# State-space scan: 5 of 16 input products on GpSimd from B rows spread by DMA, parts of B and C in a ring through DRAM, and an out-projection that alternates images

## The reference

```python
x = x + conv_branch(group_norm(x))           # 4 images, S = 1024 positions, 384 channels
t = tokens(x); t = t + attention(layer_norm(t)); t = t + experts(layer_norm(t))

def conv_branch(x):
    xh, z = split(x @ in_proj_w.T)           # 192 channels each
    xc = silu(depthwise_3x3(xh) + conv_b)
    xs = [xc by rows, xc by columns, both reversed]          # K = 4 directions
    dt, B, C = split(x_proj_w[k] @ xs[k], [24, 16, 16])      # N = 16 states
    delta = softplus(dt_projs_w[k] @ dt + dt_projs_b[k])
    for t in range(1024):                    # for each direction, channel and state n
        h[n] = h[n] * exp(delta[t] * A[n]) + delta[t] * x[t] * B[n, t]
        y[t] += C[n, t] * h[n]
    y = sum of the 4 directions, put back in order, + D * x
    y = layer_norm(y) * g + b
    return (y * silu(z)) @ out_proj_w.T      # back to 384 channels
```

## Time and profile before

| | us |
|---|---|
| median of 3 runs | 2788.26 (2787.69 to 2788.27) |
| the profiled execution's own time | 2789.66 |
| its span, first to last instruction | 2787.9 |
| TensorE matmuls busy | 2276.9 (82%) |
| TensorE weight loads busy | 1034.7 (37%) |
| VectorE busy | 1734.4 (62%) |
| ScalarE busy | 1189.9 (43%) |
| GpSimd busy | 1160.4 (42%) |
| mean granted TensorE clock | 0.927 of full |

### The profile page before, as it was taken

One profiled execution on the slowest core, in us unless ns is written; L12 is line 12 of the kernel. 1 busy time (PEld: TensorE's weight loads), 2 busy tenths in 40 slices (PEclk: granted clock), 3 DMA queues, 4 the chain that ended last, 5 costly groups with the idle time before them and its releaser, 6 DMA issues.

```text
span 2787.9 us, 21841 instructions
## 1 busy us (share of the span) xinstructions
PE 2276.9 (82%) x6404; PEld 1034.7 (37%) x6404; DVE 1734.4 (62%) x1497; ACT 1189.9 (43%) x1301; POOL 1160.4 (42%) x551
## 2 busy tenths in 40 slices
PE   4887877778787777778777776889988649999998
PEld 2333323323332333333233322444455425555554
DVE  2436999999999999999999997752122200000000
ACT  1226666666676666657666664211111111111111
POOL 0002767776676777667676764000000141111111
PEclk9988999999999999999999999789999769999999
DMA  5111000000000000000000002201011252222220
GB/s 193 56 25 44 1 0 1 0 0 0 0 0 0 0 0 0 0 0 0 0 0 0 0 0 108 83 34 45 1 45 45 92 189 101 102 104 102 104 101 17
DMA packets 44296, 111.04 MB, mean 40 GB/s; under 512 B 5168, under 2 KB 30883, under 8 KB 42978
## 3 DMA queue, kind: packets, MB, share of 16 engines
q1 hardware_dynamic: 38114, 93.59, 9.5%
q0 software_dynamic: 6144, 16.98, 1.7%
HBM read 74.68 MB, written 34.67 MB: 39 GB/s over the span
## 4 chain that ended last, share of the span: by engine, by line
PE 47%; issue 22%; DVE 18%; ACT 8%; POOL 3%; DMA 1%; DVEq 1%; SPq 0%; ACTq 0%; POOLq 0%
PE ps L975 9%; PE ps L987 9%; DVE ps L1123 8%; PE ps L756 5%; ACT arena L525 3%; POOL arena L385 3%; DVE arena L1131 3%; PE ps L700 3%; PE ps L939 2%; PE ps L737 2%; PE ps L825 2%; PE ps L864 2%; PE ps L711 2%; PE ps L727 2%; ACT arena L533 2%
## 5 line engine op out<-in xcount | busy, mean ns | idle before, releaser
L385 POOL TENSOR_TENSOR arena<-arena 128x1024 f32<-128x1024 f32 x384 | 975.5, 2540 | 438.4 <-DVE arena L1131 423.5
L1131 DVE TENSOR_TENSOR_SCAN arena<-arena,ps 128x1024 f32<-128x1024 f32 x384 | 878.1, 2287 | 13.3
L756 PE MATMUL ps<-arena 128*128 128x512 f32 x1536 | 777.9, 631 | 43.0 <-DVE arena L1110 40.1
L737 PE MATMUL ps<-arena 96*128 (+1 forms) x1536 | 424.3, 395 | 275.0 <-DVE arena L1131 236.2
L533 ACT ACTIVATE arena<-ps 128x1024 f32<-128x1024 f32 x384 | 392.4, 1022 | 437.6 <-PE ps L737 435.3
L1123 DVE TENSOR_TENSOR ps<-ps,arena 128x1024 f32<-128x1024 f32 x384 | 465.9, 1213 | 35.2 <-PE ps L737 32.7
L525 ACT ACTIVATE arena<-arena 128x1024 f32<-128x1024 f32 x384 | 438.5, 1142 | 0.3
L756 PEld LDWEIGHTS ps<-arena 128*128 128x128 f32 x1536 | 309.8, 203 | 313.6 <-issue 252.0
L737 PEld LDWEIGHTS ps<-arena 96*128 96x128 bf16 x1536 | 126.5, 100 | 688.5 <-DVE arena L1131 445.5
L1344 DVE TENSOR_TENSOR arena<-ps,arena 128x384 f32<-128x384 f32 x32 | 17.9, 558 | 450.2 <-PE ps L987 450.2
L987 PE MATMUL ps<-arena 128*128 128x384 f32 x768 | 250.2, 486 | 0.0
(11 more groups left out here) (166 smaller groups left out, 1708.6 us busy)
## 6 DMA issues: line engine op xcount, KB each, us to landing
arena<-in_w SPq DMA_DIRECT2D x16, 2304.0 KB, 16.1
slot_in<-arena SPq DMA_DIRECT2D x8, 772.0 KB, 16.0
arena<-slot_in SPq DMA_DIRECT2D x8, 772.0 KB, 18.4
arena<-in_xT SPq DMA_DIRECT2D x4, 1536.0 KB, 9.3
arena<-in_x_tok SPq DMA_DIRECT2D x1, 6144.0 KB, 21.5
tokens<-arena SPq DMA_DIRECT2D x4, 1536.0 KB, 5.8
out<-arena SPq DMA_DIRECT2D x4, 1536.0 KB, 9.6
z_scratch<-arena SPq DMA_DIRECT2D x4, 768.0 KB, 5.5
```

Source lines behind the costliest of these rows:

```text
L385: nc.gpsimd.tensor_tensor(hst[:, u % RING], hst[:, u % RING], c_sb[:, u % RING], ALU.mult).then_inc(p2_ok, 1)
L737: mm = pe.matmul(dst[:, h * 512:(h + 1) * 512], sel_lhs[0:BR, n], bc[0:BR, q // J, dr, m, h * 512:(h + 1) * 512], start=True, stop=True)
L756: mm = pe.matmul(Y_PS[:, h * 512:(h + 1) * 512], ident, hst[:, u % RING, h * 512:(h + 1) * 512], start=(u == 0), stop=(u == UN - 1))
L1131: nc.vector.tensor_tensor_scan(h, f, x, 0.0, ALU.mult, ALU.add).then_inc(sc_ok, 1)
```

## The change

- Units with n in `ON_POOL` = (2, 5, 8, 11, 14), 10 of the 32 of a tile, no longer get a B spread from TensorE nor a product from VectorE. SP loads their B row from DRAM into the unit's slot of `hst`, once for each half of the partitions, by a transfer that reads the row 64 times. GpSimd multiplies it there with `dux`, LEAD = 3 units ahead of its read-outs. Their decay goes to the unit's free buffer of `B_PS` in PSUM, when the scan of unit u-2 is done, and the scan takes decay from PSUM and input from SBUF, in place.
- `hst` has 8 slots (HRING), and LAG is 4: the addition trails by 4 units, and the evacuation comes at unit 4.
- The parts of B and C are stored to DRAM, and `bc` holds two groups in place of four; groups 2 and 3 are loaded when tiles 3 and 6 begin. A new ScalarE copy per projection step puts the B and C rows in fp32 into `rows`, which a seventh transfer stores to DRAM.
- The out-projection takes tile i of both images together, and alternates them matmul by matmul, into two banks of PSUM. Order: tiles 0 and 1, means, tile 2, squares, tile 3. VectorE's additions follow it.

```diff
-LAG = 3
+HRING = 8
+LAG = 4
+ON_POOL = (2, 5, 8, 11, 14)
+LEAD = 3
...
-        BCD = XY + 16 * S
+        BCD = XY + 12 * S
-        bc = rb.take(2 * NP, 2, 2, S, dtype=BF16)
+        bc = rb.take(2, 2, 2, S, dtype=BF16)
+        rows = rw.take(2, S)
-        hst, c_sb = rs.take(RING, S), rs.take(RING, S)
+        hst, c_sb = rs.take(HRING, S), rs.take(RING, S)
...
+            def load_bc(po):
+                sp.dma_start(bc[0:BR, po % 2], bc_dram[po]).then_inc(bc_ld, 16)
+
+            for p in range(NP):
                 for k in range(K):
...
-                            sp.dma_start(bc[part * SR:part * SR + SR, p * 2 + o, dr, m, :],
+                            sp.dma_start(bc_dram[p * 2 + o, part * SR:part * SR + SR, dr, m],
                                          parts[H2 + m * SR:H2 + m * SR + SR, k % 2, part]).then_inc(bc_st[k % 2], 16)
+                    sp.wait_ge(rows_ok, p * K + (k + 1))
+                    sp.dma_start(b_dram[p * 2 + o, dr], rows[H2:H2 + SR, k % 2]).then_inc(rows_st[k % 2], 16)
+                if p == 0:
+                    for o in range(2):
+                        sp.wait_ge(bc_st[o], 1 + K // 2 * PLACED)
+                    load_bc(0)
+                    load_bc(1)
+
+            def b_row(q, u):
+                dr, n = divmod(u, N)
+                sp.wait_ge(ya_ok, q * UN + u + 1)
+                for im in range(2):
+                    sp.dma_start(hst[H2 * im:H2 * im + H2, u % HRING],
+                                 b_dram[q // J, dr, im * N + n].partition_broadcast(H2)).then_inc(b_ld[u % HRING], 16)
...
+            for U in range(NQ * UN):
+                if U % UN in POOL_UNITS:
+                    b_row(U // UN, U % UN)
+                if U % (J * UN) == 0 and J * UN <= U < 3 * J * UN:
+                    sp.wait_ge(c_ok, U)
+                    load_bc(U // (J * UN) + 1)
...
+            def make_input(q, u):
+                dr, slot = u // N, u % HRING
+                pool.wait_ge(du_ok, q * 2 + (dr + 1))
+                pool.wait_ge(b_ld[slot], q * (32 * fed(slot)) + 32 * (fed(slot, u) + 1))
+                nc.gpsimd.tensor_tensor(hst[:, slot], hst[:, slot], dux[:, dr], ALU.mult).then_inc(in_ok, 1)
+
             def read_outs(q, last):
...
+                    if u + LEAD < UN:
+                        if u + LEAD in POOL_UNITS:
+                            make_input(q, u + LEAD)
+                    elif not last and u + LEAD - UN in POOL_UNITS:
+                        make_input(q + 1, u + LEAD - UN)
...
+                    nc.scalar.activation(rows[H2:H2 + SR, k % 2], SLOT3[k % 2][H2:H2 + SR], ACT.Copy).then_inc(rows_ok, 1)
...
-                    if not (first and u < RING):
-                        act.wait_ge(sc_ok, U + (3 - RING))
+                    kept = 2 if n in ON_POOL else RING
+                    dst = B_PS[u % 2] if n in ON_POOL else decay[:, u % RING]
+                    if not (first and u < kept):
+                        act.wait_ge(sc_ok, U + (3 - kept))
...
-                    pe.wait_ge(sc_ok, U + 1)
-                    spread(q, u, 0, B_PS[u % 2]).then_inc(b_ok, 1)
+                    if n not in ON_POOL:
+                        pe.wait_ge(sc_ok, U + 1)
+                        spread(q, u, 0, B_PS[u % 2]).then_inc(b_ok, 1)
...
+            def out_proj(c, i):
+                if i == 0:
+                    pe.wait_ge(yg_ok, 1 + c * J + J)
+                for r in range(2):
+                    pe.wait_ge(ta_ok, c * 8 + (OP_SEEN + 2 * i + r + 1 - OP_BACK[i]))
+                for j in range(J):
+                    for r in range(2):
+                        lo, hi = H2 * r, H2 * r + H2
+                        mm = pe.matmul(ps[:, op_bank(i, r), 0:C], yg[lo:hi, j, i * P:(i + 1) * P], w_out[lo:hi, j],
+                                       start=(j == 0), stop=(j == J - 1))
...
-                    dve.wait_ge(b_ok, U + 1)
-                    nc.vector.tensor_tensor(B_PS[u % 2], B_PS[u % 2], dux[:, dr], ALU.mult).then_inc(p1_ok, 1)
+                    h, slot = hst[:, u % HRING], B_PS[u % 2]
+                    if n in ON_POOL:
+                        f, x = slot, h
+                        dve.wait_ge(in_ok, q * len(POOL_UNITS) + (pool_units(u) + 1))
+                        dve.wait_ge(dec_ok, U + 1)
+                    else:
...
```

120 lines of the change are left out of this document (72 added, 48 removed).

## The result

The changed kernel takes 2711.63 us (median of 4 runs, 2708.24 to 2728.21) against 2788.27 us before: ratio 0.9737, 95% interval 0.9697 to 0.9777. The profiled execution took 2712.99 us, with a span of 2711.2. The time moved by 76.7 us, where 120 were forecast; it lies inside the range. A later comparison of the same kernel gave 2727.52 us (6 runs, 2707.47 to 2737.21; 0.9764, 0.9730 to 0.9798). Single executions of this kernel spread over 30 us, which those of before don't.

A forecast was written before the change was run, and what follows sets the result against it. VectorE, 97% busy in the scan stage, was taken as the bound; without stalls it would need 1284.9 us. Scan stage -121.8, projection +14, out-projection -12 gave -120 us, a median of 2668 us; range 2630 to 2722.

The forecast's parts named there:

- the 71 us: Scan stage: VectorE's delta work slows GpSimd's read-outs by 71 us in all, taken as unchanged; GpSimd's total 1291 us.
- boundary, with unit 6: Tile boundaries: VectorE waits for TensorE 3.5 us x 11 = 39, against 35 before: +4 (-20 to +15).
- decay through PSUM at unit 11: Scan stage: the exponential of GpSimd's unit 11 comes 0.2 us late, 23 times: +5 us (0 to 15).
- coupling, and loads of B and C: Scan stage: hiccups passed between equally loaded engines, +12 us (0 to 50); 768 KB loads ahead of a row, +6 (0 to 12).
- The core term: Scan stage: VectorE loses 10 products in each of 12 tiles, 120 x 1.24 = 148.8 us; scans stay at 2.287 us.
- GpSimd becomes the bound: Rival, chance 0.20: scan stage 1391 us in place of 1469, -78, and 2712 us with the other terms.
- Rows: Scan stage: B rows for GpSimd arrive in 4.2 us, landing taken as 3, against 6.3 us free; hidden by 2 us.
- Projection: Stage before the scans: new copy and seventh transfer +7 us, stores and loads about +7: +14 (0 to 22).
- Out-projection: After the scans: last chunk -7 us (21.3 to 15 or a little less), earlier chunks -5: together -12 (0 to -20).
- Alternating images should make that the rule: Out-projection: alternating images makes the two array halves work side by side, 0.64 us for a pair of matmuls.
- The signs listed for "right": VectorE above 93%, GpSimd above 90% busy, rows landing in 3 to 5 us, half-tiles 55 to 57, projection steps near 6.1.
- those for "wrong": Scan stage: late GpSimd inputs over 30 us, its products above 2.5, scans not 2.287, TensorE below 0.9 clock, or long exponentials.

The follow-up runs named there:

- N1: Changed kernel with GpSimd's units counted on the product's semaphore too, so all three waits before a scan compare with one value; 2723.08 us, ratio 0.9760.
- the images in turn: Changed kernel with the out-projection's three products of image 0 ahead of those of image 1, instead of alternating; 2729.29 us, ratio 0.9777.

## Why the prediction was right in sign and 43 us too far

**The step that failed** is this one: "What slows GpSimd is delta work, whose operations take both inputs from SBUF ... so I let the 71 us stand". It counted the contention on the engine that used to lose, and took VectorE's own delta operations as fixed at 0.59 + 3 x 1.12 us a half-tile. The trace of before could show it on one side only, because GpSimd idled for the scan and came second each time. With GpSimd 93% busy, VectorE comes second in most half-tiles. The same sentence priced GpSimd's total well (1291 us; L453, L439 and dux together 1312) and the loss on VectorE's side at 0 instead of 54. That these 54 us come from GpSimd's products is shown by the run without the 120 input products for 42 of them; the other 12 are argued.

The Trainium skill has this rule: SBUF — State Buffer, section Who interferes with whom, says that a VectorE instruction with two SBUF inputs contends with a GpSimd instruction that reads SBUF, that the pair of ports which both engines share is an exclusive lock, and that "Issue order, not op shape, decides who blocks." The rows agree (1.0 us to go gave 0.88 more, 0.30 gave 0.18). That an operation of VectorE waits through two further products of GpSimd that follow one another, as at 991.29, is measured here.

**The terms of the stage**, against VectorE's 1284.9 us without a stall:

| | forecast | measured |
|---|---|---|
| boundary, with unit 6 | 39.7 | 26.7 |
| decay through PSUM at unit 11 | 5 | 0.6 |
| coupling, and loads of B and C | 18 | 1.1 (what is left) |
| delta operations | 0 | 54.3 |
| pitch from product to scan | 0 | 36.7 |
| sum | 1347.6 | 1404.3 |

- The core term, 120 products x 1.24 us, held: 264 products of 1.214 us are left, and scans with decay in PSUM take 2.270 us, not the 2.287 assumed.
- One reading ahead of the forecast was off by 3 us, without effect: of the 35.2 us of idle time before products 2.5 stand ahead of the first product, outside the stage, and 32.7 in it; the other 3 of the 35.7 are the mean pitch, 1.248 us for 1.24.
- The pitch of 1.24 us was carried over from the earlier trace rows without asking what the new code puts between two instructions of a loop. N1 shows 31 of the 36.7 us to be the register; the rest is the scans of units 6 and 22 waiting for ScalarE, which N1 keeps. No row of before could price either.
- Boundary, decay, coupling: each was counted too high, 34 us together, and these hid part of the two that were missed: by luck, the forecast is nearer than its terms. The boundary's 26.7 us are a good execution's; the later profile had 21.9 more.
- GpSimd: pitch back to back 2.31 us as read from the earlier trace rows; its total and its share as forecast. The rival "GpSimd becomes the bound" gave 2712, nearly the time measured, and is still wrong: with 344 us of idle time in place of 119, GpSimd gave VectorE the delta work back and nothing more. The right number had the wrong cause.
- Rows: landing 3.9 us (2.0 to 7.3) for a forecast of 3 to 5, and 23.2 us of waits of GpSimd; VectorE's scans waited 0.6 us, and not for an input.
- Projection: +14 forecast, +1.7 measured. The steps stayed about 5.2 us apart, the new copy and the seventh transfer being hidden. Only the step after the loads shows, 9.6 us where the same step took 6.3 before. The first step began 1.8 us sooner (199.9 against 201.7), for a reason that isn't shown, so that the steps themselves cost 3.6 us:

```profile
225.58 1.00 ACT L556 ACTIVATE arena<-ps 64x1024 bf16<-64x1024 f32 x1
...
235.14 1.00 ACT L556 ACTIVATE arena<-ps 64x1024 bf16<-64x1024 f32 x1
```

- Out-projection: -12 forecast, -13.3 measured after the stage, and the nearness is luck. The last chunk gave 11.1 us for a forecast of 7: it took 10.2 us where 15 or a little less were expected, since the sum took the half clock's 0.64 us for all 24 pairs and 17 of them took 0.32. From the scan stage's end to that chunk only 1.4 us were won, for a forecast of 5; "Alternating images should make that the rule" named the wrong part of the edit, as the images in turn show.
- The signs listed for "right": VectorE above 93% (94), GpSimd above 90% (93), landing 3 to 5 us (3.9), waits at boundaries (there, but not they alone). Half-tiles came out at 58.5 us (1404.3 / 24), not 55 to 57, projection steps near 5.2, not 6.1. Of those for "wrong", none had delta operations of VectorE in it; the scans of 2.270 us met one of them, harmlessly, and the stage's clock was just above its mark of 0.9 (0.91; 0.90 in the later profile).

## What to carry to other kernels

When work moves to an idle engine that shares a port with the busy one, take every operation of the busy one that needs the port and ask which of the two will start second once the idle time is gone; contention seen from one side only is a matter of who came first. Read the mean of each operation, not only the waits, for this cost stands in busy time. In a loop, let all waits between a short operation and the next compare with one and the same value, and look for a rival that gives the same number for another reason before calling a result explained. When two stretches of TensorE are compared, compare their granted clocks first.

## What the runs showed of the hardware that was not expected

- An addition of a constant on VectorE (0.67 us) can take 6.8 us: it didn't end before GpSimd's run of products, 2.36 us each, did.
- About 0.155 us per unit between the end of an operation and the next, from a second compared value in a loop (a pitch of 1.40 to 1.41 us against 1.24 to 1.26).
- Matmuls on different halves of the array don't start strictly in the order of the program: the first for the other half started while three that stand ahead of it had not, with six in front (in turn) and with 24 (before). Six in front cost 0.7 us in 48 matmuls; with 24 in front the halves ran side by side for four pairs only.
- After an idle time of 3.2 to 3.3 us, TensorE's granted clock was 1.00 at one boundary and 0.53 on average over the next 14 us at another, in the same execution.
